# Experts' first two weight products in three rounded products instead of one fp32 product

## The chip, the cores and the metric

The kernel runs on one core of one Trainium2 chip. The time is that of a whole execution on the device in microseconds; of the kernel before there are three, with the median 2800.91 (2794.32 to 2806.15). All detail comes from one profiled execution of it.

## The reference

A graph network with two layers. Only its very end matters here, a mixture of experts on 128 tokens (M), with D = 1024, 8 experts and H = 512:

```
h1 = einsum('md,ehd->meh', x_moe, ew1) + eb1
h2 = einsum('md,ehd->meh', x_moe, ew2) + eb2
z = _ln(silu(h1) * h2, sel_ln_g, sel_ln_b)
out_all = einsum('meh,edh->med', z, ew3) + eb3
expert_out = take_along_axis(out_all, top1_idx, axis=1)
final_out = shared_out.at[index_b, index_t].set(shared_moe_out + expert_out * expert_w)
```

Beside it stands a shared branch: `sh = _ln(silu(x1) * x2)`, `shared_out = sh @ sw3`. All is float32.

## The kernel before

Weights come from memory in pieces of 128x1024 float32 (512 KB) through a ring of eight slots (`ring0` to `ring7`), issued by SyncE in the order of use. A slot is loaded again when TensorE has used its piece (`pieces_used`). For each expert there are eight pieces for the hidden stage (four with `ew1`, four with `ew2`; each holds two blocks of 128 rows by 512 columns) and four for the output stage (`ew3`).

TensorE has two ways to multiply. An fp32 product of 512 columns appears in the trace as two MATMUL records. A rounded product (operands of type fp32r) appears as one. Where the kernel uses rounded products it makes three of each: with an operand split into high (rounded) and low (the rest), it adds high x high, low x high and high x low. The dense stages before the experts work like this: ScalarE copies a piece into a rounded slot (`weights_rounded`, line 1666), and GpSimd (line 829), or for every other block of one weight VectorE (line 2093), subtracts it from the piece and leaves the rest in the ring slot (`weights_low`). The front of the kernel does the same with line 2098. GpSimd's and VectorE's subtract has two SBUF operands.

The experts use fp32 products. TensorE's order there is: hidden stage of expert 0 (`expert_hidden`, two accumulations `a` = 0 for h1 and 1 for h2, each with one rounded bias row at its end), the shared output product (16 products of the shared branch, `so`), some small jobs, then for e = 0 to 6: hidden stage of expert e+1, four transposes of z of expert e, output stage of expert e. Last come the transposes and the output stage of expert 7. The input `moe_x` (gathered tokens, ScalarE's copy of PSUM at line 1946) is the stationary operand and the weight block the moving one.

Around it: ScalarE takes the Silu of h1 (line 1956) and the square root of the variance (line 1958), in a loop over experts. VectorE multiplies Silu by h2 (line 2895), copies the transposed z out of PSUM (2940), and makes the norm of z: bn_stats (2901), scale and shift (2909), multiply by gain (2913), add (2915), and the scaling by the one-hot column (2918). Then it adds the expert's output to `e_acc` (2943, one operand in PSUM) and one block of the shared branch to the residual (2935, 2937). Before the first expert it makes the layer norm of the shared branch (`layernorm`, lines 2109 to 2136), the selection of the expert and the weights of the mixture (2848 to 2888), and after the shared output product a reciprocal and two products (2929 to 2932). GpSimd and SyncE have nothing but loads in this part.

The order is written out by hand. Every engine works through its own list, and the semaphores `product_ready` (TensorE's products), `psum_free`, `piece_in`, `to_scalar` and `from_scalar` couple them. Each engine's wait holds up all that is behind it in its list.

Of the kernel before, what the change touches and what calls it, by code (L numbers as in the profile page):

```python
# [21 lines left out]
NC2 = 2 * HC  # L22
# [184 lines left out]

AHEAD = 4
# [33 lines left out]
def gps_kernel(nc, x_tok, xT, wts, tree_w, tree_b2, tree_tab, edges, cols, mix_rows, tree, ident_rows, gate_cols, gate_rows, eb12, eb3,  # L242
# [4 lines left out]
    with ctx:  # L247
# [120 lines left out]

        low_slot = [rounded_view(f"low_{i}", f"ring{i}", 1024)[:] for i in range(RING)]
# [127 lines left out]
        bias_ready = sem("bias_ready")  # L497
        l1_sums_high = sem("l1_sums_high")
# [224 lines left out]
        def _(pool):  # L723
# [213 lines left out]
            for name, m in IN_TURN[2 * KC + AHEAD:]:  # L937
                weights_low(name, m)
            pool.wait_ge(rows_free, 1)
            for dst, src in moe_loads:  # L940
                pool.dma_start(dst, src).then_inc(rows_in, 16)


        @block.tensor
        def _(pe):
# [526 lines left out]
            def expert_hidden(e):  # L1472
                for a in range(2):
                    acc = begin()
                    for k in range(KC):
                        if k % 2 == 0:
                            w = next_piece()
                        mm(acc[:, 0:512], moe_x[:, k, :], w[:, 512 * (k % 2):512 * (k % 2) + 512],
                           k == 0, False)
                        if k % 2:  # L1480
                            held[0] += 1
# [4 lines left out]
            pe.wait_ge(eb_ready, 1)  # L1486
            expert_hidden(0)
# [56 lines left out]
        def _(act):  # L1544
# [388 lines left out]
            for c in range(HK):  # L1933
                j = JOB["shared"] + 2 * c
                if 2 * c + AHEAD < KC:
                    weights_rounded("shared", 2 * c + AHEAD)
                act.wait_ge(product_ready, j + 1)
                if c >= 2:
                    out_taken(j - 3)
                act.activation(halves((tmp_a, tmp_b)[c % 2][:, 0:NC2]), pair(j), ACT.Silu,  # L1940
                               bias=col[:, COLS["sb1"] + c:COLS["sb1"] + c + 1]).then_inc(psum_free[SLOT[j]], 1)
                if 2 * c + AHEAD < KC:
                    weights_rounded("shared", 2 * c + AHEAD + 1)
            squares(sh, sh_sq, HK)
            j = JOB["gather"]
            act.activation(moe_x.rearrange("p k m -> p (k m)"), out_ready_at(j)[:],
                           ACT.Copy).then_inc(psum_free[SLOT[j]], 1)
# [6 lines left out]
            def expert(j, turn=0):  # L1954
                act.wait_ge(product_ready, turn + (j + 1))
# [4 lines left out]
            expert(JOB["hid0"])  # L1960
            with act.Fori(0, EXPERTS // 2 - 1) as i:
                told.enter(i, 2)
                for u in range(2):
                    expert(JOB["exp"] + 4 * u, i * 8)
            told.leave(EXPERTS // 2 - 2, 2)
            expert(JOB["exp"] + 4 * EXPERTS - 8)


        @block.vector
        def _(v):  # L1970
# [135 lines left out]

            def layernorm(src, dst, kc, eps, ready, unbiased=False, affine=False):
# [4 lines left out]
                for k in range(kc):  # L2112
                    v.tensor_tensor(dst[:, k, :], src[:, k, :], mu[:], ALU.subtract).then_inc(to_scalar, 1)
                assert job.n == JOB["gather"]
# [723 lines left out]
            for c in range(HK):  # L2838
# [5 lines left out]
                                       ALU.mult).then_inc(freed(), 1)  # L2844
            v.drain()
# [99 lines left out]
            v.drain()  # L2945
            for e in range(1, EXPERTS - 1):
                expert_hidden(e % 2)
                take_turned_hidden()
                expert_norm(e, e % 2)
                take_expert()  # L2950
                add_shared(e - 1)
# [162 lines left out]
```

## Time and profile before

| What | Value |
|---|---|
| Median of three runs | 2800.91 us |
| Profiled execution | 2793.76 us |
| Its span | 2791.9 us |
| TensorE matmul busy | 2646.5 us (95%) |
| VectorE busy | 1241.0 us (44%) |
| GpSimd busy | 809.6 us (29%) |
| ScalarE busy | 607.3 us (22%) |
| Granted TensorE clock, mean | 0.977 |

The span is the part of the execution that the instructions cover. Busy time counts what ran, not what was waited for. The records of matmuls overlap in the timeline (their ends are modelled), so the spacing of starts tells more than their length. A line of the timeline merges like instructions (xN) and gives their whole stretch.

### The profile page before, as it was taken

What the parts mean: (1) busy time and instruction counts of PE and PEld (TensorE: products, weight loads), DVE (VectorE), ACT (ScalarE), POOL (GpSimd) and SP (SyncE); (2) the same over time, 40 slices, a digit from 0 to 9 for tenths busy, and PEclk for the clock granted to TensorE, in tenths of its full rate; (3) what the DMA queues carried; (4) which work ended last, traced back from release to release, by engine and by line L of the source; (5) the groups of instructions that cost most, each with busy time, mean ns of one, the idle gap of its engine ahead of it and who ended that gap; (6) DMA issues with size and microseconds to landing.
All of it is one profiled execution on the core that took longest, in us unless ns stands there. A gap on an engine that the chain in (4) does not pass through costs nothing.

```text
span 2791.9 us, 43510 instructions
## 1 busy us (share of the span) xinstructions
PE 2646.5 (95%) x14731; PEld 2194.2 (79%) x14732; DVE 1241.0 (44%) x1910; ACT 607.3 (22%) x810; POOL 809.6 (29%) x603
## 2 busy tenths in 40 slices
PE   7999899999999999979899999998979999989998
PEld 5778777799999999976677777667757879987544
DVE  8517499662322323673444444323453214433334
ACT  2222145322222221320111111201121222232010
POOL 0877789353223223321410000100011313420000
PEclk9999999999999999989899999999989999999999
DMA  5233212422212111521798989206960112113586
GB/s 215 69 88 81 51 53 96 99 71 73 59 61 70 54 56 62 219 71 37 281 357 299 347 300 342 94 0 212 327 213 15 46 61 98 61 56 100 173 277 218
DMA packets 106317, 381.29 MB, mean 137 GB/s; under 512 B 18357, under 2 KB 19092, under 8 KB 104760
## 3 DMA queue, kind: packets, MB, share of 16 engines
q1 hardware_dynamic: 83520, 301.25, 31.2%
q0 software_dynamic: 19136, 57.09, 6.8%
q10 hardware_dynamic: 3512, 20.91, 2.0%
q8 instruction: 102, 1.67, 0.2%
q14 instruction: 47, 0.38, 0.0%
HBM read 347.10 MB, written 31.77 MB: 136 GB/s over the span
## 4 chain that ended last, share of the span: by engine, by line
PE 75%; issue 8%; POOL 8%; DVE 4%; ACT 2%; DMA 2%; DVEq 1%; SPq 0%; ACTq 0%; POOLq 0%
PE pair L951 73%; POOL edge_records L740 7%; PE pair L998 2%; ACT big L1721 1%; DVE asum L2501 1%; DMA ring<-in_tree_w 1%; DVE big L2446 0%; PE pair L1136 0%; DVEq L2506 0%; DVE big L2513 0%; DMA big<-in_x_rows 0%; ACT big L1716 0%; DVE big L2444 0%; DVE big L2441 0%; ACT asum L1674 0%
## 5 line engine op out<-in xcount | busy, mean ns | idle before, releaser
L951 PEld LDWEIGHTS pair<-big,ring 128*128 128x128 f32 x3200 | 449.7, 193 | 139.2 <-issue 80.7
L951 PE MATMUL pair<-big,ring 128*128 (+1 forms) x3200 | 536.3, 320 | 13.8 <-issue 11.4
L951 PE MATMUL pair<-mean_high,low 128*128 128x314 f32 x1280 | 288.7, 307 | 0.0
L951 PE MATMUL pair<-ring,hid_plan_heads 128*125 128x512 f32 x576 | 272.6, 597 | 0.5 <-DVE hid_plan_heads L2342 0.5
L740 POOL DMA_INDIRECT edge_records<-big x160 | 207.9, 1299 | 110.4 <-issue 59.3
L2349 DVE TENSOR_TENSOR big<-pair,big 125x1024 f32 x144 | 176.3, 1225 | 107.7 <-PE pair L951 106.9
L951 PEld LDWEIGHTS pair<-mean_high,low 128*128 128x128 f32 x1280 | 212.6, 189 | 0.0
L788 POOL TENSOR_TENSOR low<-ring,high_tmp_a 128x1024 fp32r<-128x1024 f32 x36 | 97.6, 2710 | 326.2 <-ACT high_tmp_a L1812 326.2
L951 PE MATMUL pair<-ring,big 128*128 128x512 f32 x384 | 168.6, 594 | 7.9 <-DVE big L2940 7.9
L2647 DVE TENSOR_TENSOR rstd<-pair,mu 128x626 f32<-128x626 f32 x64 | 51.8, 810 | 260.7 <-PE pair L951 260.4
L951 PE MATMUL pair<-big 125*128 125x129 f32 (+10 forms) x830 | 156.3, 342 | 10.6 <-DVE big L2753 2.6
L951 PEld LDWEIGHTS pair<-big 125*128 125x128 f32 (+6 forms) x830 | 119.4, 185 | 47.0 <-issue 9.0
L756 POOL TENSOR_SCALAR asum<-iota_n,asum 128x125 bf16<-128x125 f32 x178 | 151.2, 865 | 17.1 <-PE pair L998 14.0
L951 PEld LDWEIGHTS pair<-ring,hid_plan_heads 128*125 128x125 f32 x576 | 97.2, 188 | 73.1 <-issue 71.2
L829 POOL TENSOR_TENSOR low<-ring,dense 128x1024 fp32r<-128x1024 f32 x36 | 87.0, 2422 | 231.5 <-ACT dense L1666 231.5
L1687 ACT ACTIVATE hid_plan_heads<-pair,col 128x125 f32<-128x125 f32 x144 | 52.9, 368 | 457.0 <-PE pair L951 453.9
L951 PEld LDWEIGHTS pair<-ring,big 128*128 128x128 f32 x384 | 72.2, 190 | 95.4 <-issue 85.2
L788 POOL TENSOR_TENSOR low<-ring,high_tmp_b 128x1024 fp32r<-128x1024 f32 x36 | 105.0, 2917 | 141.0 <-ACT high_tmp_b L1812 138.1
L951 PE MATMUL pair<-rel_round,x_low 125*128 125x314 f32 x560 | 127.1, 308 | 0.0
L951 PE MATMUL pair<-rel_round,x_high 125*128 125x314 f32 (+2 forms) x560 | 126.4, 307 | 0.0
L951 PE MATMUL pair<-mean_high,high_tmp_b 128*128 128x314 f32 x544 | 124.9, 311 | 0.0
L951 PE MATMUL pair<-mean_high,high_tmp_a 128*128 128x314 f32 x544 | 124.5, 310 | 0.0
(500 smaller groups left out, 4661.7 us busy)
## 6 DMA issues: line engine op xcount, KB each, us to landing
ring<-in_tree_w SPq DMA_DIRECT2D x288, 512.0 KB
ring<-in_wts SPq DMA_DIRECT2D x276, 512.0 KB
counts_spill<-big POOLq DMA_DIRECT2D x1, 5349.1 KB, 28.9
big<-in_x_rows SPq DMA_DIRECT2D x5, 512.0 KB, 8.7
xn_rows_spill<-big POOLq DMA_DIRECT2D x1, 2560.0 KB, 15.0
edge_records<-big POOLq DMA_INDIRECT x160
big<-xn_rows_spill POOLq DMA_DIRECT2D x1, 2560.0 KB, 9.9
sorted_out_q<-big POOLq DMA_DIRECT2D x5, 512.0 KB, 5.7
```

The source lines that it names most:

```text
L740: pool.indirect_dma_start(rec_dram, bass.IndirectOffsetOnAxis(ap=place_i[:, c:c + 1].bitcast(U32), axis=0), records[:, c, :], None).then_i ...
L756: ins = pool.tensor_scalar(src_hot[n % 3][:, c, 0:T], iota_n[:, 0:T], sorted_rec[:, 2 * n + c, 0:1], None, ALU.is_equal)
L788: pool.tensor_tensor(low_slot[m], ring[m][:], high_slot[m % 2].bitcast(F32), ALU.subtract).then_inc(low_ready, 1)
L829: pool.tensor_tensor(low_slot[m], ring[m][:], high_of(name, m).bitcast(F32), ALU.subtract).then_inc(dense_low, 1)
L951: ins = pe.matmul(o, lhsT, rhs, start=start, stop=stop)
L998: ins = pe.matmul(acc[0:T + 1, 512 * h:512 * h + HC], src_hot[n % 3][:, c, :], dst_hot[n % 2][:, c, HC * h:HC * (h + 1)], start=c == 0, st ...
L1687: act.activation(hid[:, parity, :], ps[SLOT[job.n]][:, 0:T], func, bias=col[:, bass.ds(g + COLS[f"{f}_b1"], 1)]).then_inc(from_scalar, 1)
L1721: act.activation(dst[:, :, T * t:T * (t + 1)].rearrange("p (h k) n -> p h k n", h=2), halves(p[:])[:, :, 0:4 * T].rearrange("p h (k n) -> ...
L2349: v.tensor_tensor(acc, wide(T), acc, ALU.add).then_inc(freed(), 1)
L2501: ins = v.tensor_scalar(dst_hot[n % 2][:, c, :], iota_h, rec[:, 1:2], None, ALU.is_equal)
L2647: v.tensor_tensor(halves(rstd[:]), product(), halves(mu[:]), ALU.mult).then_inc(freed(), 1)
```

## The change

The hidden stages of all eight experts go over to three rounded products. `moe_x` gets a rounded copy (`moe_high`, ScalarE) and a rest (`moe_low`, GpSimd). Each of an expert's eight hidden pieces i is rounded by ScalarE into its own slot `expert_slot[i]`. The rests of pieces 0, 2, 4 and 6 are taken by GpSimd, those of 1, 3, 5 and 7 by VectorE, in the ring slot. TensorE waits for the rest before the first product of a piece. The output stage stays as it was. ScalarE's loop over experts is written out.

```
+            def expert_rounded(e, i):
+                at = dense_first + expert_piece(e, i)
+                act.wait_ge(piece_in[at % RING], 16 * (at // RING + 1))
+                if e:
+                    act.wait_ge(product_ready, expert_job(e - 1, i // HK) + 1)
+                else:
+                    act.wait_ge(product_ready, AT["shared", KC - 1] + 1)
+                act.activation(expert_slot[i], ring[at % RING][:], ACT.Copy).then_inc(experts_high, 1)
...
+            for e in range(1, EXPERTS):
+                for i in range(KC):
+                    expert_rounded(e, i)
+                expert(expert_job(e, 0))
```

GpSimd and VectorE (the same helper on both, with semaphores of their own):

```
+            def expert_low(e, i):
+                pool.wait_ge(experts_high, KC * e + i + 1)
+                low = low_slot[expert_piece(e, i) % RING]
+                pool.tensor_tensor(low, ring[expert_piece(e, i) % RING][:], expert_slot[i].bitcast(F32),
+                                   ALU.subtract).then_inc(experts_low, 1)
+
+            for i in (0, 2, 4):
+                expert_low(0, i)
+            await_one(pool, JOB["gather"])
+            pool.tensor_tensor(moe_low, moe_x.rearrange("p k m -> p (k m)"), moe_high.bitcast(F32),
+                               ALU.subtract).then_inc(moe_low_ready, 1)
+            expert_low(0, 6)
...
             v.drain()
+            for i in range(1, KC, 2):
+                expert_low(1, i)
             for e in range(1, EXPERTS - 1):
                 expert_hidden(e % 2)
                 take_turned_hidden()
                 expert_norm(e, e % 2)
+                for i in (1, 3):
+                    expert_low(e + 1, i)
                 take_expert()
+                for i in (5, 7):
+                    expert_low(e + 1, i)
                 add_shared(e - 1)
```

TensorE:

```
+                    for i in range(HK * a, HK * (a + 1)):
+                        low = low_slot[piece.n % RING]
+                        next_piece()
+                        pe.wait_ge(experts_low_v if i % 2 else experts_low, HK * e + i // 2 + 1)
+                        for half in range(2):
+                            k = 2 * (i - HK * a) + half
+                            of, at = slice(P * k, P * (k + 1)), slice(512 * half, 512 * half + 512)
+                            for part, w in ((moe_high, expert_slot[i]), (moe_low, expert_slot[i]), (moe_high, low)):
+                                mm(acc[:, 0:512], part[:, of], w[:, at], k == 0 and w is expert_slot[i] and part is moe_high,
+                                   False)
+                        held[0] += 1
```

In the layer norm of the shared branch, VectorE takes rests 5 and 7 of expert 0 behind the subtractions of the mean, and rests 1 and 3 ahead of the norm:

```
                 for k in range(kc):
                     v.tensor_tensor(dst[:, k, :], src[:, k, :], mu[:], ALU.subtract).then_inc(to_scalar, 1)
+                for i in (5, 7):
+                    expert_low(0, i)
                 assert job.n == JOB["gather"]
```

VectorE, from the last bias of an expert's norm to the next expert, before (z is `tmp_b`; lines 2935 and 2937 add a shared block):

```order
L2907 RECIPROCAL small<-small 128x1
L2909 TENSOR_SCALAR tmp_b<-tmp_b,small 128x512
L2913 TENSOR_TENSOR tmp_b<-tmp_b,big 128x512
L2915 TENSOR_TENSOR tmp_b<-tmp_b,big 128x512
L2918 TENSOR_SCALAR tmp_b<-tmp_b,small 128x512
L2943 TENSOR_TENSOR big<-pair,big 128x1024
L2935 SCALAR_TENSOR_TENSOR big<-rstd,big 128x626
L2937 TENSOR_TENSOR big<-big 128x626
L2895 TENSOR_TENSOR tmp_b<-pair,tmp_a 128x512
```

The same place after; `low_85<-ring,expert_71` is the rest of piece 1:

```order
L2972 TENSOR_SCALAR tmp_b<-tmp_b,small 128x512
L2976 TENSOR_TENSOR tmp_b<-tmp_b,big 128x512
L2978 TENSOR_TENSOR tmp_b<-tmp_b,big 128x512
L2981 TENSOR_SCALAR tmp_b<-tmp_b,small 128x512
L2163 TENSOR_TENSOR low_85<-ring,expert_71 128x1024
L2163 TENSOR_TENSOR low_87<-ring,expert_73 128x1024
L3006 TENSOR_TENSOR big<-pair,big 128x1024
L2163 TENSOR_TENSOR low_81<-ring,expert_75 128x1024
L2163 TENSOR_TENSOR low_83<-ring,expert_77 128x1024
L2998 SCALAR_TENSOR_TENSOR big<-rstd,big 128x626
L3000 TENSOR_TENSOR big<-big 128x626
L2958 TENSOR_TENSOR tmp_b<-pair,tmp_a 128x512
```

Four subtracts of 128x1024 have come between the expert's scaling and the next product, two before the expert's output is taken and two after. GpSimd, at the start of the experts, after (before, only the two loads stand here):

```order
L963 TENSOR_TENSOR low_80<-ring,expert_70 128x1024
L963 TENSOR_TENSOR low_82<-ring,expert_72 128x1024
L963 TENSOR_TENSOR low_84<-ring,expert_74 128x1024
L969 TENSOR_TENSOR moe_low<-big,moe_high 128x1024
L963 TENSOR_TENSOR low_86<-ring,expert_76 128x1024
L974 DMA big<-in_sel_rows 128x1024
L974 DMA big<-in_eb 8x1024
L963 TENSOR_TENSOR low_84<-ring,expert_70 128x1024
L963 TENSOR_TENSOR low_86<-ring,expert_72 128x1024
L963 TENSOR_TENSOR low_80<-ring,expert_74 128x1024
L963 TENSOR_TENSOR low_82<-ring,expert_76 128x1024
```

Its first four subtracts and the input's rest belong to expert 0, the next four to expert 1, and four for each expert follow in the same way. ScalarE, the end of one expert after (roundings 3 to 7 of eight; before, only the table loads, the Silu into `tmp_a` and the square root into `small`):

```order
L1993 ACTIVATE expert_73<-ring 128x1024
L1993 ACTIVATE expert_74<-ring 128x1024
L1993 ACTIVATE expert_75<-ring 128x1024
L1993 ACTIVATE expert_76<-ring 128x1024
L1993 ACTIVATE expert_77<-ring 128x1024
L2011 ACT_TABLE_LOAD
L2011 ACTIVATE tmp_a<-pair 128x512
L2013 ACT_TABLE_LOAD
L2013 ACTIVATE small<-small 128x1
```

The eight roundings of an expert stand between the square root of the expert before and its own Silu.

## Rows read from the trace of the kernel before

**Rows 1.** The profile page, part 4, engines of the chain that ended last.
```profile
PE 75%; issue 8%; POOL 8%; DVE 4%; ACT 2%; DMA 2%; DVEq 1%; SPq 0%; ACTq 0%; POOLq 0%
```

**Rows 2.** Timeline of one expert: start us, us, engine, line, operation [idle before].
```profile
2647.28 0.19 PEld L951 LDWEIGHTS pair<-eb_rows,eb_signs 128*128 128x128 f32 x1 [0.24 <-issue]
...
2648.22 0.69 DVE L2895 TENSOR_TENSOR tmp_b<-pair,tmp_a 128x512 f32<-128x512 f32 x1 [11.45 <-PE pair L951]
...
2649.56 14.00 PE L951 MATMUL pair<-ring,big 128*128 128x512 f32 x32 [1.01 <-DVE big L2940]
...
2650.81 0.20 ACT L1958 ACTIVATE small<-small 128x1 f32<-128x1 f32 x1 [7.87 <-DVE small L2905]
...
2651.91 0.69 DVE L2913 TENSOR_TENSOR tmp_b<-tmp_b,big 128x512 f32<-128x512 f32 x1
...
2652.68 0.69 DVE L2915 TENSOR_TENSOR tmp_b<-tmp_b,big 128x512 f32<-128x512 f32 x1
...
2653.45 0.49 DVE L2918 TENSOR_SCALAR tmp_b<-tmp_b,small 128x512 f32<-128x512 f32 x1
```

**Rows 3.** Timeline, where expert 1's hidden stage begins.
```profile
2610.96 7.03 PE L951 MATMUL pair<-ring,big 128*128 128x512 f32 x16
...
2615.87 0.86 DVE L2932 SCALAR_TENSOR_TENSOR big<-big,small,mu 128x626 f32<-128x626 f32 x1
```

**Rows 4.** Timeline of TensorE, two bias rows of the dense stage.
```profile
2280.97 0.62 PE L951 MATMUL pair<-bias_rows,bias_signs 128*125 128x512 f32 x2
...
2292.60 0.62 PE L951 MATMUL pair<-bias_rows,bias_signs 128*125 128x512 f32 x2
```

**Rows 5.** Timeline, a weight load and the rounding of its piece.
```profile
2185.08 0.33 SPq L668 DMA_DIRECT2D ring<-in_wts  x1
...
2188.56 1.06 ACT L1666 ACTIVATE dense<-ring 128x1024 fp32r<-128x1024 f32 x1 [2.64 <-DMA ring<-in_wts]
```

**Rows 6.** Instruction groups by shape: xcount, busy us, mean ns, idle before.
```profile
L829 POOL TENSOR_TENSOR low<-ring,dense 128x1024 fp32r<-128x1024 f32 x36 | 87.0, 2422 | 231.5 <-ACT dense L1666 231.5
...
L2098 DVE TENSOR_TENSOR low<-ring,front 128x1024 fp32r<-128x1024 f32 x15 | 17.7, 1219 | 13.4 <-issue 10.0 <-ACT front L1653 3.4
...
L2647 DVE TENSOR_TENSOR rstd<-pair,mu 128x626 f32<-128x626 f32 x64 | 51.8, 810 | 260.7 <-PE pair L951 260.4
```

**Rows 7.** Timelines, GpSimd and VectorE at work side by side.
```profile
588.27 2.39 POOL L788 TENSOR_TENSOR low<-ring,high_tmp_b 128x1024 fp32r<-128x1024 f32 x1 [1.65 <-ACT high_tmp_b L1812]
...
588.53 2.15 DVE L2603 TENSOR_SCALAR big<-iota_n,big 4x8 f32<-4x8 f32 x1
...
596.04 5.26 DVE L2649 TENSOR_TENSOR big<-big,rstd 128x626 f32<-128x626 f32 x1
...
1183.36 9.10 POOL L788 TENSOR_TENSOR low<-ring,high_tmp_b 128x1024 fp32r<-128x1024 f32 x1 [4.57 <-ACT high_tmp_b L1812]
...
2260.64 5.73 POOL L829 TENSOR_TENSOR low<-ring,dense 128x1024 fp32r<-128x1024 f32 x2 [1.87 <-ACT dense L1666]
...
2261.54 5.91 DVE L2093 TENSOR_TENSOR low<-ring,dense 128x1024 fp32r<-128x1024 f32 x2 [0.55 <-ACT dense L1666]
```

**Rows 8.** Timeline and window (busy us, granted clock, DMA) after an idle stretch.
```profile
2141.24 0.53 PE L951 MATMUL pair<-sums_high,high_tmp_a 128*128 128x314 f32 x2 [3.50 <-DVE normed_low L2077]
...
2142.00:2146.00 4.00, 4.00 (x19) 4.00 (x18) 3.91 (x5) 0.00 (x0) 0.00 (x0) 0.57 0.00 0
```

**Rows 9.** Timeline around expert 0.
```profile
2551.71 1.02 ACT L1946 ACTIVATE big<-pair 128x1024 f32<-128x1024 f32 x1 [4.29 <-PE pair L951]
...
2555.93 0.81 DVE L2122 TENSOR_SCALAR rstd<-pair 128x626 f32<-128x626 f32 x1 [9.28 <-PE pair L951]
...
2557.44 7.11 PE L951 MATMUL pair<-ring,big 128*128 128x512 f32 x16
...
2564.97 1.91 DVE L2136 TENSOR_SCALAR big<-big,col 128x626 f32<-128x626 f32 x4
```

**Rows 10.** Window of the tree stage: busy us, granted clock, DMA share, GB/s.
```profile
1400.00:1450.00 50.00, 50.00 (x285) 36.18 (x284) 22.03 (x28) 5.47 (x15) 6.66 (x7) 1.00 0.96 359
```

More of the change, by code:

```diff
@@ L206, with expert_piece, expert_job @@
 LOW_BY_POOL = [b for b in HIGH_ORDER if b not in LOW_BY_VECTOR]
+def expert_piece(e, i):
+    return KC * len(DENSE) + 12 * e + i
+def expert_job(e, a):
+    return JOB["exp"] + 4 * (e - 1) + a if e else JOB["hid0"] + a
 AHEAD = 4
@@ L367, in high_of @@
             return dense_slot[5, IN_TURN.index((name, m)) % AHEAD]
+        expert_slot = [rounded_view(f"expert_{i}", "big", 1024, at)[:] for i, at in enumerate(
+            [1024 * i for i in range(5)] + [5120 * 6 + 1024 * i for i in range(3)])]
+        moe_high, moe_low = (rounded_view(f"moe_{n}", "big", 1024, 5120 * 5 + HK * NC2 + 1024 * i)[:]
+                             for i, n in enumerate(("high", "low")))
         low_slot = [rounded_view(f"low_{i}", f"ring{i}", 1024)[:] for i in range(RING)]
@@ L497, in gps_kernel @@
         bias_ready = sem("bias_ready")
+        experts_high = sem("experts_high")
+        experts_low = sem("experts_low")
+        experts_low_v = sem("experts_low_v")
+        moe_low_ready = sem("moe_low_ready")
         l1_sums_high = sem("l1_sums_high")
@@ L941, in _ @@
                 pool.dma_start(dst, src).then_inc(rows_in, 16)
+            for e in range(1, EXPERTS):
+                for i in range(0, KC, 2):
+                    expert_low(e, i)
         @block.tensor
@@ L1486, in _ @@
             pe.wait_ge(eb_ready, 1)
+            pe.wait_ge(moe_low_ready, 1)
             expert_hidden(0)
@@ L1952, in _, with expert @@
             act.activation(mix_w, pair_s, ACT.Exp).then_inc(from_scalar, 1)
-            def expert(j, turn=0):
-                act.wait_ge(product_ready, turn + (j + 1))
+            def expert(j):
+                act.wait_ge(product_ready, j + 1)
                 act.activation(tmp_a[:, 0:HID], ps[SLOT[j]][:, 0:HID], ACT.Silu).then_inc(psum_free[SLOT[j]], 1)
@@ L1958, in expert @@
                 act.activation(c0, c0, ACT.Sqrt).then_inc(from_scalar, 1)
[L1960 to L1966, printed above, removed]
+            expert(expert_job(0, 0))
+            for e in range(1, EXPERTS):
+                for i in range(KC):
+                    expert_rounded(e, i)
+                expert(expert_job(e, 0))
         @block.vector
@@ L2105, in xn_rest, with expert_low @@
                                 ALU.subtract).then_inc(front_x_low, 1)
+            def expert_low(e, i):
+                v.wait_ge(experts_high, KC * e + i + 1)
+                low = low_slot[expert_piece(e, i) % RING]
+                v.tensor_tensor(low, ring[expert_piece(e, i) % RING][:], expert_slot[i].bitcast(F32),
+                                ALU.subtract).then_inc(experts_low_v, 1)
             def layernorm(src, dst, kc, eps, ready, unbiased=False, affine=False):
@@ L2844, in _ @@
                                        ALU.mult).then_inc(freed(), 1)
+            for i in (1, 3):
+                expert_low(0, i)
             v.drain()
@@ L2949, in _ @@
                 expert_norm(e, e % 2)
+                for i in (1, 3):
+                    expert_low(e + 1, i)
                 take_expert()
+                for i in (5, 7):
+                    expert_low(e + 1, i)
                 add_shared(e - 1)
```

16 lines of the change are left out of this document (7 added, 9 removed).

## Prediction

> **What bounds the kernel now.** I read the chain of waits first: 75% of it is TensorE, so time saved there counts as long as nothing else becomes late [rows 1]. In the stage that changes I read the timeline of one expert, because experts 2 to 7 repeat the same pattern. Call the end of an expert's hidden stage (both products and both bias rows) zero. The second bias row's weights load at 2647.28; that row itself runs from 0.43 to 0.66 us later, when the product ahead of it is through, so zero is 2647.94 [rows 2]. VectorE's product follows at +0.3, the second-layer (output) product of the expert before starts at +1.75 (2649.69, its weights from 2649.56), and ScalarE's square root ends at +3.07 (2650.81 + 0.20) [rows 2]. A group of 16 records of fp32 products with 512 columns lasts 7.03 us, of which the last record is 0.59: (7.03 - 0.59) / 15 = 0.429 us apiece, two to a product [rows 3]. The output stage is 16 of them, 6.86 us, so the next hidden stage starts at +8.6. It has 32 such records and two bias rows, 13.73 + 0.46 = 14.2 us. The period is 22.8 us, and TensorE waits in it only about 1 us, for VectorE's copy [rows 2]. No weight is waited for.
>
> **TensorE's own gain.** Rounded products of 512 columns stand in the trace: from one bias row at 2280.97 to the next at 2292.60 there are 50 of them, 11.63 / 50 = 0.2326 us each [rows 4]. A hidden stage becomes 48 + 2 of them, 11.63 us instead of 14.2: 2.55 us less per expert, 20.4 us for eight. The stationary blocks load beside the products, as there. (128 stationary columns rather than 125 is the only difference; I price it at nothing, at most 0.01 us a product, 4 us in all.)
>
> **What is added, and when it can start.** Per expert: eight roundings on ScalarE of 1.06 us [rows 5], four rests on GpSimd of 2.42 us, four on VectorE of 1.22 us [rows 6]. None can be early. ScalarE's queue has the roundings of expert e+1 behind the square root of expert e, so they run from +3.1: piece 0 is rounded at 4.2, piece 1 at 5.3, piece 2 at 6.3, piece 3 at 7.4, piece 4 at 8.4. TensorE wants piece 0 at 8.6 and each next one 1.4 us later (six products of 0.2326).
>
> The question is whether GpSimd and VectorE can make rests at the same time. The trace says no [rows 7]. VectorE's add of two SBUF operands lasts 5.26 us at 596.04, while GpSimd makes rests; a tensor_scalar over 4x8 elements lasts 2.15 us at 588.53, until GpSimd's subtract from 588.27 ends; GpSimd's subtract at 1183.36 lasts 9.10 us instead of 2.4 beside a row of VectorE's two-operand adds; and two rests on each side, asked for together, take from 2260.64 to 2267.45, 6.8 us, near the 4.8 + 2.4 that all four need one after another, and each side is lengthened. VectorE's product of the same size with one operand in PSUM has a mean of 0.81 us over 64 of them [rows 6], so it never waited. So I count rests, and VectorE's SBUF-only multiply, add and final scaling, as excluding each other, the waiting side getting the next turn, as at 2260.64.
>
> The Trainium skill, SBUF — State Buffer, section "Who interferes with whom", says that VectorE and GpSimd share one pair of ports under an exclusive lock, which a VectorE instruction takes with two SBUF inputs or in a two-port mode, tensor_scalar among them. The trace agrees (5.26 us at 596.04). By that rule the scaling must wait too, as I count it; without it for the scaling, the result is the second rival below.
>
> **One expert, worked through** (VectorE's multiply 3.97 to 4.66, add from 4.74, scaling from 5.51 now [rows 2]):
> - GpSimd rest 0: ready 4.2, waits for the multiply, 4.7 to 7.0.
> - VectorE add waits, 7.0 to 7.7; GpSimd rest 2: 7.7 to 10.1.
> - VectorE scaling waits, 10.1 to 10.5; GpSimd rest 4: 10.5 to 12.9.
> - VectorE rest 1, queued behind the scaling: 12.9 to 14.0. TensorE wanted it at 10.0 and waits 4.1 us. Behind that wait on TensorE are all later products and nothing that another engine needs sooner.
> - GpSimd rest 6: 14.0 to 16.4; VectorE rest 3: 16.4 to 17.5, wanted at 14.1 + 2.8 = 16.9, a wait of 0.7.
> - Rests 5 and 7 by 21.2, in time (20.6 is when 5 could be wanted; it is ready at 20.0).
>
> Waits of 4.9 against a gain of 2.55: each of the experts 2 to 7 is 2.35 us longer, 14.1 us together. The bounds: with no exclusion every rest is in time and an expert gains the 2.55; if GpSimd twice keeps its turn against a waiting VectorE (the 5.26 us at 596.04 is the add's 0.81 and 4.45 of waiting, nearly two subtracts), rest 1 ends at 16.6 and the expert is 4.0 longer. I take 2.35, nearest to the pattern at 2260.64.
>
> **Expert 1.** Its odd rests stand on VectorE behind the whole chain of the mixing weights, whose last instruction is at 2615.87 for 0.86 us, while TensorE begins this hidden stage at 2610.96 [rows 3]. Rest 1 is ready at 2618.2, TensorE wants it at 2612.4: 5.8 us of waiting, the others follow in time. Less 2.55: +3.3. GpSimd has made its rests long before, so nothing excludes anything here.
> After an idle stretch of 3.50 us before 2141.24 the granted clock has a mean of 0.57 over the 4 us from 2142 [rows 8] (0.50 would be 1.2 GHz all through, 1.00 is 2.4), though TensorE is busy in all of them: 4 x 0.43 = 1.7 us lost. I add 1.7 for the 5.8 us of waiting here. For the 4.1 us in the other experts I add nothing, and at most 0.9 each (the slowed pieces use up the 0.7 wait of piece 3).
>
> **Expert 0.** Its hidden stage ends 2.55 us earlier, if the rests are in time: rests 0 to 4 lie beside the sums and the gather, and rest 1 is early enough. But what comes next waits for the shared layer norm ("sh", four instructions from 2564.97, 1.91 us), and two rests now stand ahead of its scale at 2555.93 [rows 9]. ScalarE's gather copy (2551.71, 1.02 us), its new rounded twin and roundings 5 to 7 end at 2557.0; GpSimd has the input's rest and rest 6 in between, so VectorE's rest 7 ends at 2561.0: the norm is 5.0 us late and ends at 2571.9, where the next stage began at 2571.7 before. Net +0.1, the gain is lost. If rests did not exclude each other it would be 2.4 late and the stage would start 2.5 earlier.
>
> **Supply.** 12 pieces of 512 KB in 25.1 us is 251 GB/s, less than now (276); even at 20.2 us it would be 311, and 359 GB/s is moved from 1400 to 1450 [rows 10]. Pieces 4 to 7 are asked for when the output stage frees slots, from +3.5; a load asked for at 2185.08 is rounded from 2188.56 [rows 5], 3.5 us, so piece 4 is there by 7.4, when ScalarE comes to it. I price supply at nothing. The Silu of an expert now stands behind eight roundings, the last ending near +13; its product ends at +19. Covered.
>
> **The sum.** 0.1 + 3.2 + 1.7 + 14.1 = +19 us. The profiled execution took 2793.76 us (its span is 2791.9), so 2812.9. It is 7.2 us under the median of the three runs, 2800.91, so the forecast against that median is 2820.
>
> **Rivals.**
> - *No exclusion worth the name.* For it: GpSimd's rests of the dense stage have a mean of 2.42 us, though VectorE works beside them [rows 6]. Against: [rows 7]. Then -2.55 for expert 0, +3.2 and 1.7 for expert 1, -2.55 x 6 = -15.3: -13, 2788. This is faster, by just under half a per cent.
> - *Only two-operand instructions exclude.* The scaling then runs at 7.8, rest 1 gets the turn at 10.1 and ends at 11.3, rests 3 and 5 are 0.7 and 0.5 late; 2.6 of waiting eats the 2.55. What is left is expert 1: +5, 2806, no change. Against it: the 2.15 us tensor_scalar, though it is small (4x8).
> - *The slower side:* GpSimd keeps the turn twice in every expert (24 us instead of 14.1), or the clock falls after each 4.1 us wait (6 x 0.9): 2825 to 2830. It decides the moment idle stretches of 4 us bring the clock down as 3.5 did.
> - *The change does not save on TensorE:* with the 0.01 us per product above or more, 4 us on top of any case.
>
> **Chances.** Forecast case 0.54 (own range 2812 to 2828), no exclusion 0.14, two-operand only 0.17, slower side 0.15. The range that leaves out two in ten is 2794 to 2832. What a measurement can tell from no change is 0.5%, 14 us: 2787 to 2815. Faster takes half of the first rival and a little luck elsewhere, 0.13; the same has the rest of it, the second rival and the low end of the forecast, 0.27; slower 0.60.
>
> **What would show it.** In the new profile: products of 0.2326 us spacing in the hidden stages; TensorE waiting 4 us for VectorE's rest before piece 1 of experts 2 to 7 and about 0.7 before piece 3; 5.8 us once in expert 1; VectorE's add and scaling of the expert norm lengthened from 0.69 and 0.49 to about 3; rests on VectorE of 3.5 us; an expert's period of 25.1 us; the stage after hidden 0 starting at the same time as before. I am wrong if those instructions keep their lengths, if the period is below 22.8, or if TensorE's wait is for the loads.

## The result: 0.4% slower, and the profile after

The changed kernel has a median of 2811.3 us (2804.4 to 2814.6), the kernel before, on the same chips, of 2799.7 us (2794.3 to 2806.2): a ratio of 1.004, 95% interval [1.0029, 1.0051]. The forecast was 2820 us in a range of 2794 to 2832. The sign is right, the size is not: 11.5 us against 19. By the bound of half a per cent this is "the same", which had 0.27, not "slower", which had 0.60. In what follows one execution of the kernel where rest 4 waits (3361.6 us) and one of the kernel before (3031.0) ran at a low granted clock throughout, 0.74 and 0.84, and the ratios leave them out.

The spans of the profiled executions differ by more, 2809.8 against 2791.9, because part of the difference lies in work that the change does not touch. The products that sum the shared network's output are the last that start before a new instruction can hold TensorE up. I use their start as a mark in every kernel. Timelines of TensorE, the kernel before first:

```profile
2538.27 4.46 PE L951 MATMUL pair<-big,ones 128*128 128x313 f32 x16 [1.19 <-issue]
```
```profile
2542.42 4.46 PE L987 MATMUL pair<-big,ones 128*128 128x313 f32 x16 [1.19 <-issue]
```

4.15 of the 17.9 us come ahead of the mark. It stands between 2539.9 and 2546.0 in the other ten kernels that were profiled, and the kernel before was profiled in one of its fastest executions (2793.8 us; the nine timed ones go from 2794.3 to 2806.2). I take this part as scatter of executions; no run shows it apart. From the mark to the end the kernel before has 253.6 us and the changed one 267.4: **13.8 us more**, near the 11.5 of the medians. They divide like this (us):

| stretch | before | after | difference | forecast |
|---|---|---|---|---|
| mark to the stage after expert 0 (2571.71 and 2575.58) | 33.44 | 33.16 | -0.3 | +0.1 |
| that stage to expert 1's first product (2610.96 and 2618.02) | 39.25 | 42.44 | +3.2 | 0 |
| expert 1's hidden stage (to 2625.16 and 2636.68) | 14.20 | 18.66 | +4.5 | +4.9 |
| experts 2 to 7 (to 2761.84 and 2779.78) | 136.7 | 143.1 | +6.4 | +14.1 |
| the rest | 30.1 | 30.0 | 0.0 | 0 |

The chain of waits answers to [rows 1]: TensorE 72% where it was 75, VectorE 8% where it was 4.

```profile
PE 72%; issue 8%; POOL 8%; DVE 8%; ACT 2%; DVEq 1%; DMA 1%; SPq 0%; ACTq 0%; POOLq 0%
```

The waits of TensorE from 2560 on (us in total, times, longest). The first and the third line are new: VectorE's rests, at ten places, and the shared norm, which ends too late, at one.

```profile
PE pair L987 <- DVE low L2163: 19.2, 10, 5.2
PE pair L987 <- DVE big L3003: 7.9, 8, 1.0
PE pair L987 <- DVE big L2197: 2.1, 1, 2.1
...
```

**Expert 1 and the clock.** Timeline of the changed kernel where expert 1's hidden stage starts, against [rows 3]:

```profile
2614.43 2.45 PE L987 MATMUL pair<-big,ones 128*128 128x313 f32 x4
...
2622.69 0.86 DVE L2995 SCALAR_TENSOR_TENSOR big<-big,small,mu 128x626 f32<-128x626 f32 x1
2623.62 4.63 DVE L2163 TENSOR_TENSOR low<-ring,expert 128x1024 fp32r<-128x1024 f32 x4
2624.99 0.77 PE L987 MATMUL pair<-expert,moe_high 128*128 128x512 f32 x1 [5.19 <-DVE low L2163]
2625.56 0.63 PE L987 MATMUL pair<-expert,moe_low 128*128 128x512 f32 x1
```

VectorE's rest 1 stands behind the last instruction of the mixing weights, as forecast; TensorE waits 5.19 us. The product behind it lasts 0.63 us where one at full speed has 0.40. Windows of the changed kernel (us, busy of PE, PEld, DVE, ACT, POOL, granted clock, DMA share, GB/s) show the lower level, 0.50 or 1.2 GHz, at six places behind the mark; in the kernel before the mean from 2560 to 2790 is 1.00.

```profile
2577.00:2580.00 3.00, 3.00 (x7) 1.89 (x7) 1.76 (x11) 1.05 (x3) 0.09 (x1) 0.50 0.90 292
2615.00:2617.00 2.00, 2.00 (x5) 1.33 (x4) 0.84 (x2) 0.00 (x0) 0.00 (x0) 0.50 0.68 254
2625.00:2627.00 2.00, 2.00 (x5) 1.62 (x6) 2.00 (x2) 0.00 (x0) 0.00 (x0) 0.50 0.15 16
2697.00:2699.00 2.00, 2.00 (x6) 1.51 (x6) 2.00 (x2) 1.13 (x1) 1.30 (x1) 0.50 0.74 258
2721.00:2723.00 2.00, 2.00 (x6) 1.53 (x5) 2.00 (x3) 1.86 (x2) 1.99 (x1) 0.50 0.31 72
2768.00:2771.00 3.00, 3.00 (x7) 2.38 (x8) 3.00 (x3) 2.76 (x3) 2.02 (x1) 0.50 0.40 120
```
```profile
2560.00:2790.00 230.00, 218.73 (x600) 110.40 (x598) 93.07 (x159) 28.65 (x35) 1.10 (x2) 1.00 0.67 222
```

Five of the six come behind a wait of 2.08 to 5.19 us. The second comes behind a wait of 1.04 us, which the kernel before (third line below) has too, there without a fall.

```profile
2575.58 35.76 PE L987 MATMUL pair<-big,ring 128*128 128x313 f32 x128 [2.08 <-DVE big L2197]
```
```profile
2612.49 2.01 PE L987 MATMUL pair<-big 8*128 8x512 f32 x4 [1.04 <-DVE big L2988]
```
```profile
2606.84 1.98 PE L951 MATMUL pair<-big 8*128 8x512 f32 x4 [1.04 <-DVE big L2925]
```

The first two falls make the +3.2 of the second line of the table: the 33.8 us from the stage's start to the transpose of the one-hot (the selection of the expert) became 35.6, and the 5.4 from there to expert 1 became 6.8.

**Experts 2 to 7** fall into two patterns. Their periods (from one hidden stage's end to the next) are 22.43, 22.40, 25.43, 25.18, 22.41 and 25.25 us; before it was 22.8. A period belongs to the expert whose hidden stage it ends with, and its zero is the end of the hidden stage before. First expert 2 (its zero is 2636.68), a short one; compare [rows 2]:

```profile
2640.64 0.69 DVE L2976 TENSOR_TENSOR tmp_b<-tmp_b,big 128x512 f32<-128x512 f32 x1
2640.77 5.56 POOL L963 TENSOR_TENSOR low<-ring,expert 128x1024 fp32r<-128x1024 f32 x2 [30.37 <-ACT expert L1993]
2641.41 2.69 DVE L2978 TENSOR_TENSOR tmp_b<-tmp_b,big 128x512 f32<-128x512 f32 x1
...
2644.18 2.44 DVE L2981 TENSOR_SCALAR tmp_b<-tmp_b,small 128x512 f32<-128x512 f32 x1
2645.41 1.06 ACT L1993 ACTIVATE expert<-ring 128x1024 fp32r<-128x1024 f32 x1 [1.41 <-DMA ring<-in_wts]
2646.54 4.55 DVE L2163 TENSOR_TENSOR low<-ring,expert 128x1024 fp32r<-128x1024 f32 x2
2646.55 3.46 POOL L963 TENSOR_TENSOR low<-ring,expert 128x1024 fp32r<-128x1024 f32 x1 [0.21 <-ACT expert L1993]
...
2647.90 0.47 PE L987 MATMUL pair<-expert,moe_high 128*128 128x512 f32 x1 [1.06 <-DVE low L2163]
```

The add lasts 2.69 us instead of 0.69 and the scaling 2.44 instead of 0.49, beside GpSimd's rests 0 and 2. That is the turn taking that the forecast took from [rows 7]. The Trainium skill, SBUF — State Buffer, section "Who interferes with whom", says that a VectorE instruction with two SBUF inputs contends with GpSimd's reads and that a tensor_scalar can contend with it; these rows agree (2.69 and 2.44 us). But GpSimd's rest 2 ends at 2646.33 and ScalarE's rounding of piece 4 only at 2646.47, since it waited 1.41 us for the load. GpSimd has nothing to do at that moment, so VectorE's rest 1 goes first and TensorE waits 1.06 us. By the starts of its products TensorE loses 1.3 us here, 0.55 before piece 3 and 0.3 before piece 5: 20.24 us (the period without waits, from the first experiment) and 2.2 are the 22.4. Then expert 5 (its zero is 2706.94), a long one:

```profile
2711.03 8.06 POOL L963 TENSOR_TENSOR low<-ring,expert 128x1024 fp32r<-128x1024 f32 x3 [12.73 <-ACT expert L1993]
...
2715.28 1.06 ACT L1993 ACTIVATE expert<-ring 128x1024 fp32r<-128x1024 f32 x1 [1.22 <-DMA ring<-in_wts]
2716.80 4.50 DVE L2163 TENSOR_TENSOR low<-ring,expert 128x1024 fp32r<-128x1024 f32 x2
...
2720.31 0.77 PE L987 MATMUL pair<-expert,moe_high 128*128 128x512 f32 x1 [3.24 <-DVE low L2163]
```

Here piece 4 is rounded by 2716.34, before rest 2 is over, and GpSimd makes rests 0, 2 and 4 without a gap. Rest 1 comes behind them, TensorE waits 3.24 us, and the clock falls. Counted from each zero, rounding 4 ends at 9.8, 10.1, 9.4, 9.4, 9.95 and 9.66 us in the six experts; rest 2 ends at 9.65 in the three short ones. The three that are clearly later are the short periods. Of the long ones, experts 5 and 7 are as shown; in expert 4 rest 0 had come ahead of the multiply as well, which lasted 2.69 us, so that VectorE was a turn behind from the start.

### The profile page after: what moved, and what is told of

The parts are those of the page before. It is cut to its first block, busy times and chain, and to the rows that moved or that the text cites. A ratio compares the mean times of both kernels' runs of the same rounds, so it can differ in the third digit from the quotient of the medians.

```text
span 2809.8 us, 43990 instructions
## 1 busy us (share of the span) xinstructions
PE 2645.2 (94%) x14859; PEld 2229.7 (79%) x14860; DVE 1330.7 (47%) x1942; ACT 671.9 (24%) x875; POOL 900.0 (32%) x636
## 4 chain that ended last, share of the span: by engine, by line
PE 72%; issue 8%; POOL 8%; DVE 8%; ACT 2%; DVEq 1%; DMA 1%; SPq 0%; ACTq 0%; POOLq 0%
PE pair L987 70%; POOL edge_records L760 7%; PE pair L1034 1%; DVE low L2163 1%; ACT big L1762 1%; DVE asum L2562 1%; DVE tmp_b L2978 1%; DVE tmp_b L2981 1%; DVE big L2507 0%; PE pair L1172 0%; DVE big L2574 0%; DVEq L2567 0%; DMA big<-in_x_rows 0%; ACT big L1757 0%; DVE big L2505 0%
## 5 line engine op out<-in xcount | busy, mean ns | idle before, releaser
L987 PEld LDWEIGHTS pair<-big,ring 128*128 128x128 f32 x3200 | 455.6, 195 | 139.9 <-issue 79.4
L987 PE MATMUL pair<-big,ring 128*128 (+1 forms) x3200 | 542.6, 323 | 14.1 <-issue 9.6
L963 POOL TENSOR_TENSOR low<-ring,expert 128x1024 fp32r<-128x1024 f32 x32 | 88.2, 2769 | 143.8 <-ACT expert L1993 143.8
L987 PE MATMUL pair<-mean_low,high_tmp_b 128*128 128x314 f32 x544 | 122.5, 306 | 0.0
## 6 DMA issues: line engine op xcount, KB each, us to landing
xn_rows_spill<-big POOLq DMA_DIRECT2D x1, 2560.0 KB, 13.8
```

Of the source, the lines that this page charges most:

```text
L963: pool.tensor_tensor(low, ring[expert_piece(e, i) % RING][:], expert_slot[i].bitcast(F32), ALU.subtract).then_inc(experts_low, 1)
L987: ins = pe.matmul(o, lhsT, rhs, start=start, stop=stop)
```

## The experiments

Theory A, from the prediction and the profile: the rests come late because GpSimd and VectorE exclude each other and take turns, and each longer wait of TensorE also costs clock. Rival B: something else is late (loads, roundings) or lengthens the instructions (traffic). The times from the mark to the end of the profiled execution, which leave the scatter ahead of it out, stand beside the medians at the end of this section. The experiments ran in three groups, each on a chip of its own with the kernel before beside it; its medians there are 2798.8, 2799.2 and 2797.6 us, so medians of different groups compare to 1 or 2 us only, and the ratios are the safer figures.

**No rests at all.** GpSimd's and VectorE's rests of the expert weights are left out, and the third product reads the rounded piece. This kernel leaves a term of the sum out and serves only to price the rests.

```
-    pe.wait_ge(experts_low_v if i % 2 else experts_low, HK * e + i // 2 + 1)
+    pe.wait_ge(experts_high, KC * e + i + 1)
+    low = expert_slot[i]
...
```

> Leaves out the thirty-two rests of the expert weights on each of GpSimd and VectorE: the third product of each block reads the rounded piece instead, and TensorE waits for ScalarE's roundings alone. The number of TensorE's products is that of the changed kernel. Theory A (the rests come late, because GpSimd and VectorE take turns at one resource, and each wait of TensorE above about 2 us is followed by some 3.3 us at half clock): no waits for rests, expert period 22.8 - 2.55 = 20.2 us, multiply, add and scaling of the norm back at 0.69, 0.69 and 0.49 us, the stage after expert 0 begins 2.5 us earlier than in the kernel before, no clock falls: 8 x 2.55 = 20 us under the kernel before, 2780 us. Rival B (roundings and loads are what is late): TensorE then waits for ScalarE's rounding of pieces 4 to 7, the period stays at 22 us or more, 2795 us or more.

Measured: 2778.3 us, 0.9931 [0.9914, 0.9947]. The waits of TensorE from 2560 on have no line for ScalarE or a load:

```profile
PE pair L981 <- DVE big L2994: 7.9, 8, 1.0
PE pair L981 <- DVE big L2979: 1.0, 1, 1.0
...
```

The period is 20.24 us in all six experts (22.8 - 2.55 = 20.25). So products, roundings and loads together are worth the 20 us that the arithmetic gives, and the rests take them and 12 more. Rival B falls as far as supply goes. One thing was not expected: the clock still fell once, for 3 us at 2608.

**Expert 1's VectorE rests early.**

```
     for m in range(KC):
         v.tensor_scalar(halves(B2[:, m, :]), product(), bias("sb3", m), None, ALU.add)...
+        for i in {0: (1, 3), 4: (5,)}.get(m, ()):
+            expert_low(1, i)
     ...
     v.tensor_scalar(halves(mu[:]), product(), 1.0, None, ALU.max)...
+    expert_low(1, 7)
```

> The changed kernel with VectorE's four rests of expert 1 taken as their pieces are rounded, between the evictions of the shared network's second layer and ahead of the reciprocal of the mixing weights. Theory A: the 5.19 us wait and the 1.3 us lost to the clock behind it are gone, 6.5 us less than the changed kernel: 2805 us. Rival (piece 7, rounded last at 2618, and the supply set the start): the wait only moves to a later piece of expert 1, under 2 us gained.

Measured: 2804.0 us, 7.3 below the changed kernel (6.8 from the mark to the end); 1.0022 [1.0009, 1.0035] of the kernel before. The 5.19 us wait is gone and no other took its place in expert 1; the clock stays up there. Theory A's term holds.

**All rests of experts 1 to 7 on VectorE.** GpSimd's loop over them is left out, VectorE takes 0 to 3 behind the norm's scaling and 4 to 7 behind the addition to the sum (expert 1's early, as above).

```
-    for i in (1, 3):
+    for i in range(4):
         expert_low(e + 1, i)
     take_expert()
-    for i in (5, 7):
+    for i in range(4, KC):
         expert_low(e + 1, i)
```

> The changed kernel with all eight rests of experts 1 to 7 on VectorE, none on GpSimd; expert 0 as it was. Theory A (the lengthening is the turn taking between the two engines): add 0.69 us, scaling 0.49, every rest 1.22; all rests in time, period 20.2 us for experts 2 to 7 where the changed kernel has 143.1 / 6 = 23.85, so 22 us less there, and 6.5 less in expert 1: 2811 - 28 = 2783 us, faster than both kernels. Rival B (the lengthening comes from SBUF traffic of loads and TensorE, not from GpSimd): the rests stay at 2.3 to 3.4 us, eight of them take 18 to 27 us of an expert, TensorE waits more than now: 2815 to 2840 us.

Measured: 2783.7 us, 0.9947 [0.9926, 0.9968], faster than both kernels though VectorE does twice as many rests. Groups of this kernel from 2630 to 2750 (xcount, busy us, mean ns, idle before):

```profile
L2163 DVE TENSOR_TENSOR low<-ring,expert 128x1024 fp32r<-128x1024 f32 x48 | 56.4, 1221 | 3.7 <-ACT expert L1993 3.6
...
L2976 DVE TENSOR_TENSOR tmp_b<-tmp_b,big 128x512 f32<-128x512 f32 x6 | 4.2, 692 | 0.5
L2978 DVE TENSOR_TENSOR tmp_b<-tmp_b,big 128x512 f32<-128x512 f32 x6 | 4.2, 692 | 0.4
L2981 DVE TENSOR_SCALAR tmp_b<-tmp_b,small 128x512 f32<-128x512 f32 x6 | 2.9, 486 | 0.5
```

and of the changed kernel from 2637 to 2760:

```profile
L963 POOL TENSOR_TENSOR low<-ring,expert 128x1024 fp32r<-128x1024 f32 x21 | 58.0, 2774 | 93.0 <-ACT expert L1993 93.0
...
L2163 DVE TENSOR_TENSOR low<-ring,expert 128x1024 fp32r<-128x1024 f32 x20 | 37.6, 1921 | 0.0
...
L2978 DVE TENSOR_TENSOR tmp_b<-tmp_b,big 128x512 f32<-128x512 f32 x6 | 16.2, 2695 | 0.4
L2981 DVE TENSOR_SCALAR tmp_b<-tmp_b,small 128x512 f32<-128x512 f32 x5 | 12.2, 2433 | 0.4
```

Without GpSimd's rests the add is back at 0.69 us, the scaling at 0.49 and the rests at 1.22, at the same loads and the same products. This is the run that shows the exclusion: traffic would have left them long. All six periods are 20.2 us.

**Products that nobody reads, in two waits.** Nine ahead of the wait for the shared norm, 22 ahead of expert 1's wait; each is a copy of the bias row's product into columns that nobody uses or that the next product starts anew.

```
     expert_hidden(0)
+    acc = begin()
+    for _ in range(9):
+        mm(acc[:, 0:512], eb_signs[:, 0:P], eb_rows[:, 0:HID], True, True)
     pe.wait_ge(operands_ready, stage("sh"))
     ...
+    if (e, i) == (1, 1):
+        for _ in range(22):
+            mm(acc[:, 512:1024], eb_signs[:, 0:P], eb_rows[:, 0:HID], True, True)
```

> The changed kernel with products whose result nobody reads in two places where TensorE waits: 9 before the wait for the shared norm (2.08 us of waiting), 22 before the wait for expert 1's first VectorE rest (5.19 us). Each is a bias row's product of 0.233 us. Theory A (a wait brings the granted clock down): TensorE does not stand still there, the clock stays at 1.00 behind both places; 1.8 us less up to the one-hot's transpose (from 35.6 to 33.8) and 1.3 less in expert 1: 2808 us. Rival (the clock falls for another reason, as the rounded products' power or a clock elsewhere): the granted clock still shows 0.50 behind both places, 2811 us.

Measured: 2813.3 us, 1.0049 [1.0033, 1.0066]. Windows of this kernel over both places:

```profile
2573.00:2583.00 10.00, 9.95 (x40) 7.17 (x39) 7.62 (x31) 4.67 (x6) 1.08 (x2) 1.00 0.69 245
...
2618.00:2632.00 14.00, 14.00 (x63) 11.34 (x62) 7.64 (x7) 2.09 (x3) 0.00 (x0) 1.00 0.50 146
```

The clock stayed at 1.00 at both, where the changed kernel has 0.50: theory A's mechanism is shown. The time was missed all the same (the interval is not apart from the changed kernel's), and in the profile not by the fillers: experts 2 to 7 of this execution had five long periods and one short one (25.24, 25.26, 26.45, 22.4, 25.3, 25.15), 149.8 us instead of 143.1. From the mark to the end of expert 1's hidden stage this kernel has 90.8 us where the changed one has 94.3, the 3 us that were expected; they are lost in how the turns fall behind it. The period of 26.45 us has a wait of 3.59 us and then 7 us at the lower clock.

**GpSimd's rest 4 behind VectorE's rest 1.** One wait more.

```
     for e in range(1, EXPERTS):
         for i in range(0, KC, 2):
+            if e > 1 and i == 4:
+                pool.wait_ge(experts_low_v, HK * e + 1)
             expert_low(e, i)
```

> The changed kernel with one wait more: GpSimd starts rest 4 of experts 2 to 7 only when VectorE's rest 1 of that expert is done. Theory A (two patterns stand in the changed kernel: a period of 22.4 us where rest 1 gets its turn ahead of rest 4, and one of 25.2 where rest 4 is ready first, with 3.2 us of waiting and 1.7 lost to the clock): all six experts show the short period, 6 x 22.42 = 134.5 us instead of 143.1, 8.6 us less: 2803 us. Rival (the load of pieces 3 and 4 is late in the long ones, and rest 4 only follows it): long periods stay, 2808 us or more.

Measured: 2799.6 us, 11.7 below the changed kernel and not to be told from the kernel before, 0.9997 [0.9986, 1.0008]. Timeline of expert 2's rests:

```profile
2647.83 2.44 DVE L2983 TENSOR_SCALAR tmp_b<-tmp_b,small 128x512 f32<-128x512 f32 x1
2650.20 2.35 DVE L2165 TENSOR_TENSOR low<-ring,expert 128x1024 fp32r<-128x1024 f32 x2
2651.49 6.67 POOL L963 TENSOR_TENSOR low<-ring,expert 128x1024 fp32r<-128x1024 f32 x2 [1.49 <-DVE low L2165]
2651.55 0.47 PE L989 MATMUL pair<-expert,moe_high 128*128 128x512 f32 x1 [1.07 <-DVE low L2165]
```

All six periods are 21.55 to 21.96 us, none long, and no clock fall in them. Waiting made the kernel faster, more than expected: GpSimd held back until rest 1 was done lets rest 3 through too, and the losses before pieces 3 and 5 (0.55 and 0.3 us) are gone. Experts 2 to 7 take 13.4 us less than in the changed kernel, and expert 1 takes 1.5 more, since its clock stayed down for 7 us. The rival (a late load behind the long ones) falls: in the long ones the load was early.

**VectorE's rests 1, 3 and 5 ahead of the norm's multiply, add and scaling.**

```
+    for i in ahead:                # (1, 3, 5), experts 2 to 7
+        expert_low(e + 1, i)
     v.tensor_tensor(z, z, sel_gb[:, 0:HID], ALU.mult)
     ...
     take_expert()
+    expert_low(e + 1, 7)
```

> The changed kernel with VectorE's rests 1, 3 and 5 of experts 2 to 7 ahead of the multiply, add and scaling of the expert norm instead of behind them; the split over the two engines as it was. Theory A (the two engines take turns, and a turn that VectorE spends on the norm is followed by one of GpSimd): rest 1 ends 8.1 us after the hidden stage, where TensorE wants it at 10; rests 3 and 5 in time; 0 to 0.7 us of waiting for rest 6: period 20.2 to 20.9 us, 143.1 - 6 x 20.6 = 19.5 us less than the changed kernel, no clock falls in these experts: 2792 us. Rival (GpSimd keeps the resource while it has rests ready, whatever VectorE asks for): rest 1 comes behind rests 0, 2 and 4 as in the slower experts, period 24 us or more, 2811 us or more.

Measured: 2804.5 us, 1.0024 [1.001, 1.0037]: 6.8 below the changed kernel, not 19.5. Rest 1 is in time, as theory A had it, so the rival (GpSimd keeps its turn, 2811 us or more) falls. But I had not followed the queue to its end. Rest 7 now stands behind multiply, add, scaling and the addition to the sum:

```profile
2650.01 2.89 DVE L2978 TENSOR_TENSOR tmp_b<-tmp_b,big 128x512 f32<-128x512 f32 x1
...
2652.97 0.69 DVE L2980 TENSOR_TENSOR tmp_b<-tmp_b,big 128x512 f32<-128x512 f32 x1
...
2655.28 1.22 DVE L2163 TENSOR_TENSOR low<-ring,expert 128x1024 fp32r<-128x1024 f32 x1
...
2656.64 0.47 PE L987 MATMUL pair<-expert,moe_high 128*128 128x512 f32 x1 [1.97 <-DVE low L2163]
```

The periods are 22.5 to 23.6 us. The wait moved from piece 1 to piece 7 (1.97, 0.36, 2.01, 2.01, 1.06 and 1.99 us), which neither theory had. Behind the first and the fourth of these the clock fell for 6 to 7 us, behind the others it did not; windows of this kernel:

```profile
2658.00:2663.00 5.00, 4.22 (x10) 2.29 (x9) 3.22 (x8) 1.15 (x3) 0.00 (x0) 0.50 0.31 106
...
2700.00:2712.00 12.00, 8.98 (x28) 4.65 (x27) 9.73 (x14) 4.82 (x6) 3.61 (x2) 1.00 0.65 233
```

**Expert 0's rests all on GpSimd.** `expert_low(0, ...)` is taken out of VectorE's queue (1, 3 ahead of the shared norm, 5, 7 inside it) and stands on GpSimd as 0 to 4 and, behind the input's rest, 5 to 7.

> The changed kernel with all eight rests of expert 0 on GpSimd, none on VectorE; experts 1 to 7 as they were. Theory A (VectorE's rests make the shared norm late, TensorE waits 2.08 us for it and the clock falls behind that): the norm ends before the hidden stage of expert 0 does, the 2.08 us wait is gone and the clock stays at 1.00 at the start of the next stage: 2.1 + 1.8 = 3.9 us less than the changed kernel, 2807 us. Rival (the roundings on ScalarE ahead of the norm's square root, and GpSimd's turns against the norm's own instructions, make it late): the wait stays above 1 us, under 1 us gained.

Measured: 2808.7 us, 1.0037 [1.0026, 1.0048]. The interval is not apart from the changed kernel's, so the medians alone show no gain; the profile shows it where the edit is. From the mark to the end of expert 1's hidden stage this kernel has 90.8 us instead of 94.3, 3.5 less where 3.9 were expected; behind the last product, where the two kernels are the same, its profile is 1.1 us longer, for which I have no cause. TensorE stands still for 0.3 us instead of 2.08 before the norm's products, and the clock stays up behind it. The norm still ends 2.7 us later than before (31.3 us behind the mark against 28.6). Its four subtractions, 2.98 us in the kernel before, take turns with the rests, and ScalarE takes the norm's square root only behind them and its own roundings, as the rival had it.

```profile
2551.45 8.80 DVE L2176 TENSOR_TENSOR big<-big,mu 128x626 f32<-128x626 f32 x4
```

**Both together, and beyond.** Expert 0's rests on GpSimd, all others on VectorE.

> Expert 0's rests all on GpSimd, those of experts 1 to 7 all on VectorE: the two edits measured one by one, together. Theory A: the gains add, 3 to 4 us below the kernel with VectorE alone for experts 1 to 7: 2780 us, 0.7% faster than the kernel before. Rival (expert 0's norm is late anyway): as that kernel, 2784 us.

Measured: 2779.8 us, 0.993 [0.9913, 0.9946], as expected. The clock fell once behind the wait of 1.04 us for the transposed one-hot, now for 7 us. So four products that nobody reads went into that wait:

```
     pe.transpose(acc[0:EXPERTS, 0:P], onehot, ident[:]).then_inc(product_ready, 1)
     job.next()
+    acc = begin()
+    for _ in range(4):
+        mm(acc[:, 0:512], eb_signs[:, 0:P], eb_rows[:, 0:HID], True, True)
     await_one(pe, JOB["onehotT"])
```

> The kernel with expert 0's rests on GpSimd and all others on VectorE, plus 4 products that nobody reads (0.93 us in all) while TensorE waits 1.04 us for the copy of the turned one-hot. In every kernel with rounded experts the granted clock stood at 0.50 for 3 to 7 us just behind this place, in the kernel before it did not. Theory A (the idle stretch there brings the clock down): the clock stays at 1.00 from 2605 to 2620, 2 to 3 us less than without the products: 2777 us. Rival (it is the light work around it, 8-row operands and short loads, or what ran 30 us earlier): the clock still falls, 2780 us.

Measured: **2776.1 us, 0.9933 [0.9917, 0.9948]**, the lowest median. Window of the kernel without the four (first) and with them:

```profile
2610.00:2616.00 6.00, 6.00 (x13) 3.99 (x13) 4.28 (x4) 2.34 (x2) 0.00 (x0) 0.50 0.24 87
```
```profile
2607.00:2617.00 10.00, 10.00 (x40) 7.14 (x39) 8.30 (x6) 2.68 (x3) 0.00 (x0) 1.00 0.43 149
```

The mechanism holds in this one profile. That the four products alone make the kernel faster is not shown: the two intervals overlap almost wholly.

Last, all rests of all experts on VectorE: of expert 0, 0 to 3 ahead of the shared norm, 4 behind its subtractions, 5 to 7 while it waits for its square root.

> All rests of all eight experts on VectorE, 0 to 4 of expert 0 ahead of and behind the shared norm's subtraction, 5 to 7 while the norm waits for its square root. GpSimd makes only the rest of the input. Theory A: nothing takes turns, the norm's four subtractions are back at 2.98 us (8.8 with GpSimd's rests beside them), the norm is no later than with GpSimd: 2779 to 2780 us, as with expert 0 on GpSimd. Rival (seven more rests in VectorE's queue make the norm 2 us late, and the clock falls): 2783 to 2784 us.

Measured: 2780.0 us, 0.994 [0.9926, 0.9953]. The subtractions are back at 2.97 us, and TensorE waits 0.3 us for the norm, as with expert 0 on GpSimd. In this stage sharing between the engines gained nothing that these runs can tell.

| kernel | median us | mark to end us | kernel before beside it, median us |
|---|---|---|---|
| before | 2799.7 | 253.6 |  |
| changed | 2811.3 | 267.4 | 2799.7 |
| no rests | 2778.3 | 235.0 | 2798.8 |
| expert 1 early | 2804.0 | 260.6 | 2798.8 |
| 1 to 7 on VectorE | 2783.7 | 239.2 | 2798.8 |
| products in two waits | 2813.3 | 270.6 | 2798.8 |
| rest 4 waits | 2799.6 | 255.6 | 2799.2 |
| rests first | 2804.5 | 261.8 | 2799.2 |
| expert 0 on GpSimd | 2808.7 | 264.9 | 2799.2 |
| both | 2779.8 | 237.4 | 2799.2 |
| both, four products | 2776.1 | 234.1 | 2797.6 |
| all on VectorE | 2780.0 | 235.3 | 2797.6 |

## Why the prediction was right in sign and wrong in size

- *TensorE's own gain, 2.55 us an expert:* right. The period without waits is 20.24 us, and the rival that 128 stationary columns cost more falls.
- *Exclusion between the engines, read from [rows 7]:* right, and shown by the run that empties GpSimd. The rivals of no exclusion and of the scaling running free fall (2.44 us instead of 0.49).
- *Experts 2 to 7, +2.35 us each:* this step was mis-sized: +6.4 us in all instead of +14.1. What failed is the line "piece 4 is rounded at 8.4", with supply priced at nothing. The loads were no bound, but a small lateness decided the turns: ScalarE waited 1.0 to 1.8 us for piece 4 (in expert 2 it was there at 8.7 us, not by 7.4), and rounding 4 ended at 9.4 to 10.1 us, about when rest 2 did (9.65). In three experts GpSimd missed its turn and rest 1 waited 1.06 us rather than 4.1. In the other three it came as forecast, with 3.23 to 3.40 us. That a later arrival could help was no case of mine at all.
- *No clock cost in these experts:* wrong by its own rival. Each long one lost 25.2 - 20.24 - 3.4 = 1.6 us behind its wait (3.4 is the wait by the starts of the products; the records, whose ends are modelled, give 3.24), more than the 0.9 that I allowed. Forecast and measured long periods agree (25.1 and 25.2) by luck: the wait was overestimated by about what the clock took. The slower rival's condition (idle stretches of this length bring the clock down) was met, in three experts.
- *Expert 1:* +4.5 measured against +4.9. By the starts of the products the wait was 5.35 us (5.19 in the records) instead of 5.8, the clock took 1.4 behind it instead of 1.7, and 0.2 at the stage's start were left over from the fall ahead: 5.35 + 1.43 + 0.24 - 2.55 = 4.47.
- *Expert 0:* -0.3 against +0.1. The norm's scale was 4.5 us late instead of 5.0 (2564.59 against [rows 9], less the 4.15 of the mark). But here too I left out the clock: TensorE's 2.08 us of standing still cost 1.8 us in the next stage, which I had treated as the same in both kernels, and 1.4 more were lost ahead of expert 1. These 3.2 us had no term.

The errors have opposite signs: 7.7 us too much in experts 2 to 7, 3.2 too little in between.

## What to carry to other kernels

Work that goes to two engines to be done sooner has to be costed with what they exclude: here 4 x 2.42 + 4 x 1.22 = 14.6 us of turns did worse than 8 x 1.22 = 9.8 us on one engine. Where two engines take turns, follow the times at which each next operand arrives to a tenth of a microsecond, or force the order with a wait: a wait for the piece that is needed first gained 11.7 us. And a wait of TensorE of two or three microseconds has to be priced with the clock that can fall behind it, here 1.4 to 1.8 us.

## What the runs showed of the hardware

- In the changed kernel the granted clock was down at 0.50 for 3 to 4 us behind waits of 2.08, 3.23, 3.24, 3.40 and 5.19 us, at a cost of 1.4 to 1.8 us each. How long it stays down varies: 7 us behind the 5.33 us of expert 1 in the kernel where rest 4 waits, and behind 3.59 us in the kernel with products in two waits.
- The length of the wait alone does not decide it. In the kernel with rests first the clock fell behind waits of 1.97 and 2.01 us and stayed at 1.00 behind two others of 2.01 and 1.99 us.
- It also fell behind a wait of only 1.04 us among light products (8-row operands) in the profiles of ten of the eleven kernels with rounded experts, all but the one with four added products there, and not in the kernel before, which has the same wait. Why it falls there stays open; the run without any rests had the fall too.
- A tensor_scalar over 128x512 fp32 from SBUF to SBUF on VectorE waits for GpSimd's subtraction like a two-operand instruction (2.44 us instead of 0.49). A reciprocal over 128x626 does not: it kept its 4.07 us in the midst of three of GpSimd's rests, and they their 2.38 each. Timeline of the kernel with expert 0 on GpSimd and the others on VectorE:

```profile
2560.57 7.13 POOL L963 TENSOR_TENSOR low<-ring,expert 128x1024 fp32r<-128x1024 f32 x3
...
2563.08 4.07 DVE L2182 RECIPROCAL rstd<-rstd 128x626 f32<-128x626 f32 x1 [3.20 <-ACT rstd L1600]
```
